# A fused attention, expert, scan and ternary layer stack: step sizes of the scan in one bundle, uncut steps, planner weights of its own for the first and last sequences, and three PSUM banks for the first attention

## The chip, the core and the metric

The kernel runs on one core of one Trainium2 chip. That core has five engines with a queue each: TensorE (PE, with weight loads, PEld, beside it), VectorE (DVE), ScalarE (ACT), GpSimd (POOL) and SyncE (SP), which issues the DMAs here. Each queue runs in order. The metric is the device time of one execution in microseconds (us).

## What is computed

Eight sequences of 512 rows by 256 columns go through four residual blocks. Cut to what matters:

```python
x = x + layernorm(attention(layernorm(x)))   # bf16, 2 heads, relu on q, k, v and output
x = x + layernorm(experts(layernorm(x)))     # 8 experts of 176 and a shared one, top 2 by sqrt(softplus(.)) + bias
x = x + layernorm(state_space(layernorm(x))) # f32, below
x = x + layernorm(ternary_ffn(layernorm(x))) # f32, hidden 1024, relu squared, rms norm

# state_space, per sequence: 512 channels, 16 states each, 512 time steps
z, xb, B, C, dt = split(h @ W_in.T)
delta = softplus(dt @ W_dt.T + 2 * b_dt)     # the step sizes
u = silu(conv4(repeat(xb)) + conv_b)
state = exp(delta * A) * state + delta * u * B
y = (sum(state * C) + u * D) * silu(z)
out = y @ W_out.T
```

## The kernel before, in words

**Chains.** The work of a sequence is cut into steps that are put into rounds: EARLY (attention, norms, the gate of the experts), LATE (experts, two norms, input projection, convolution, step sizes), GATE and BACK (z, gating, output projection, ternary layers, store). A round is begun only when every step of the round before it has been taken.

**The scan.** The 512 channels stand in four tiles of 128 partitions, with 16 states each: 64 scan steps per sequence, each over 128 x 512. For each, PE spreads a row of B over the partitions (L966), DVE multiplies it by `du` (L1437), ACT makes `exp(delta * A)` (L1171), DVE scans (L1430), POOL multiplies the state by C (L1453), and PE adds the product into `ps_y` (L973). After 16 of them, DVE takes the tile's sum (L1443, "taken").

**Planner.** `weave` writes each engine's order at build time. It walks a clock with a cost for every step (tables `BUSY` and `SCAN_BUSY`, in units of 10 ns). At each turn it gives the engine to the step that can start first; those that can start within one unit of it are told apart by urgency: the rest of a chain times a weight by eighth of the chain (`URGENT`, or `FIRST` for the first iteration), against a weight for the scan. The orders are fixed, and semaphores alone hold the engines together on the chip.

**Iterations.** Iteration n weaves the scan of sequence n, LATE of n+1, EARLY of n+2, BACK of n-1 and GATE of n. Iterations 1 to 4 are a loop, 0, 5, 6 and 7 are written out. Ahead of them EARLY of sequence 0 runs alone (with the quantising of the ternary weights beside it), then LATE of 0 is woven with EARLY of 1 until `du` of its tile 0 is planned; what is left of both is held over into iteration 0, where LATE of 1 and EARLY of 2 are begun only once both are through. After iteration 7, BACK of sequence 7 runs alone. Iteration 6 has no EARLY, iteration 7 neither EARLY nor LATE.

**Step sizes.** For each tile i there are ten steps: `d` (PE, L899), `d_abs` (ACT, two instructions, L1108 and L1109), `d_exp`, `d_one`, `d_less`, `d_log` (ACT, one each, L1112 to L1123), `d_fix`, `d_sum`, `delta`, `du` (POOL, L1477 to L1488). `d_log` needs another activation table than the exponentials. `d_abs` of tiles 0 to 2 waits until the scan of the sequence before has taken the same tile (`free_slot`, and `CROSS` in the planner); tile 3 has two slots in turn. The tiles come one after another, in the order 0, 3, 1, 2, each nine rounds after the last:

```python
    for i in range(CT):
        k = 15 + 9 * D_AT[i]
        steps += [(k, "P", ("d", i)), (k + 1, "A", ("d_abs", i)), (k + 2, "A", ("d_exp", i)), (k + 3, "A", ("d_one", i)),
```

**Halves.** `halved` gives the long steps (`proj`, `gram`, `fc`, `wout` on PE, `x4` and `apply` on ACT, `add` and `gate_root` on POOL, the store on SP) a first half `..._a`, so that the planner may put other work between. Matmuls and activations are the same in number either way; each POOL `add` and `gate_root` is two instructions of half the size, each store two DMAs of 256 KB.

**First attention.** In EARLY every product of PE goes into the one PSUM bank `XE`, and the next waits until ACT has copied the last out (`EARLY_BANK`).

Of the kernel before, what the change touches and what calls it, by code (L numbers as in the profile page):

```python
# [49 lines left out]


D_ORDER = (0, CT - 1) + tuple(range(1, CT - 1))
D_AT = tuple(D_ORDER.index(i) for i in range(CT))

# [103 lines left out]
def late_rounds():  # L158
# [30 lines left out]
def back_rounds():  # L189
# [8 lines left out]
    for t in range(NT):  # L198
        r += [[("P", ("proj", t))], [("P", ("gram", t))], [("A", ("p_out", t))]]
        if t == 2:  # L200
# [3 lines left out]
          [("V", ("o", "shift"))], [("A", ("o", "apply"))], [("G", ("o", "add"))], [("S", "store_a"), ("S", "store")]]  # L204
# [13 lines left out]
def quant_rounds():  # L218

    r = []  # L220
    for w in range(2):
# [3 lines left out]
        for h in range(2):  # L225
# [4 lines left out]

FIRST_HALF = {"proj": "proj_a", "gram": "gram_a", "fc": "fc_a", "wout": "wout_a", "x4": "x4_a", "apply": "apply_a", "add": "add_a",
              "gate_root": "gate_root_a"}


def first_half(e, step):

    if isinstance(step, str):
        return FIRST_HALF.get(step)
    name, i = step
    if name in FIRST_HALF:  # L240
        return FIRST_HALF[name], i
# [16 lines left out]
def places(rounds):  # L258

    at = {}  # L260
    for r in rounds:
        for e, step in r:
# [6 lines left out]
    "A": {"b_turned": 91, "back apply_a": 98, "back apply": 98, "c_out": 48, "cw_turned": 48, "d_abs": 114, "d_exp": 54, "d_less": 61,  # L269
          "d_log": 54, "d_one": 52, "dt_out": 48, "eps16": 19, "exp": 122, "f_turned": 48, "gate_abs": 17,  # L270
          "gate_exp": 12, "gate_log": 14, "h_turned": 91, "late apply_a": 94, "late apply": 94, "p_out": 38, "probs": 122, "pv_out": 48,
          "qk_out": 48, "raw": 48, "relu": 49, "round": 20, "shift": 123, "square": 53, "tanh": 49, "turned": 91,
          "v_out": 48, "v_relu": 96, "w_out": 48, "wo_out": 48, "wo_relu": 96, "x4_a": 112, "x4": 112, "x_one": 52, "x_tanh": 57,
          "x_turned": 91, "y_turned": 91, "z_tanh": 49},
    "G": {"add_a": 110, "add": 110, "d_fix": 123, "d_sum": 122, "delta": 122, "du": 123, "gate_root_a": 270, "gate_root": 270, "gated_y": 123,
          "rms": 98, "root": 98, "rstd": 98},
    "P": {"b_turn": 45, "bm": 70, "c": 130, "conv": 96, "cw_turn": 25, "d": 96, "down": 131, "dt": 130, "f_turn": 44,
          "fc_a": 96, "fc": 96, "gate": 60, "gram_a": 89, "gram": 89, "h_turn": 45, "proj_a": 173, "proj": 173, "pv": 86, "qk": 43, "scores": 22,
          "turn": 45, "up1": 45, "up3": 45, "v": 44, "weigh": 32, "wo": 44, "wout_a": 173, "wout": 173, "x_turn": 45, "xs": 130,
          "y_turn": 45, "z": 130},  # L280
    "V": {"add": 60, "aggr": 24, "b_hi": 34, "b_lo": 54, "b_mid": 20, "b_rest": 52, "back stats": 109, "center": 78,
          "divide": 78, "early stats": 130, "gate_eq": 33, "gate_gt": 34, "gate_low": 33, "gate_or": 33,
          "gate_rank": 31, "gate_sum": 11, "gate_twin": 18, "gated": 60, "gram_pick": 61, "late stats": 98,
          "max": 113, "ms": 60, "qk_bias": 53, "scale": 34, "silu": 60, "stats0": 66, "u": 66, "v_bias": 60,
          "weighted": 60, "wo_bias": 60, "z_silu": 60},
}
SCAN_BUSY = {"decay": 62, "spread": 33, "drive": 60, "scan": 114, "product": 123, "pair": 122, "sum": 96, "taken": 66, "load": 6}


TABLE_LOAD = 128  # L290
LOG_TABLE = ("log",)
USES = {"d_log": "log", "gate_log": "log", "d_exp": "exp", "gate_exp": "exp", "exp": "exp", "decay": "exp",
        "tanh": "tanh", "x_tanh": "tanh", "z_tanh": "tanh"}
# [13 lines left out]
def busy(e, kind, step):  # L307

    n, of = name_of(step), BUSY.get(e, {})
    return of.get(n, of.get(kind + " " + n, 6 if e == "S" else 9))  # L310
# [12 lines left out]
def scan_entries(e, j, part):  # L323
# [23 lines left out]
    elif e == "S" and part == 0 and (j < 0 or 1 <= j <= PER - 5):  # L347
# [11 lines left out]
FIRST = {"late": (42.9, 24.5, 7.37, 44.6, 3.04, 338, 3.77, 11),  # L359
          "early": (2.05, 15.5, 0.226, 0.444, 0.464, 5.13, 0.419, 47.2),  # L360
          "back": (0.342, 0.491, 0.571, 0.801, 0.855, 0.521, 0.922, 0.117),
          "scan": (134, 39.9, 69.3, 11.5, 39.2, 17, 25.5, 3.42)}
# [1495 lines left out]
```

## Time and profile before

| what | value |
|---|---|
| median of 3 runs | 1937.45 us (1933.76 to 1938.24) |
| the profiled execution | 1933.68 us |
| its span, first to last instruction | 1931.9 us |
| mean granted TensorE clock | 0.925 of full speed |
| PE busy | 1602.0 us (83%) |
| DVE busy | 1545.5 us (80%) |
| ACT busy | 1208.3 us (63%) |
| POOL busy | 1001.8 us (52%) |

Shares are means over stages with different limits; the table by stage stands with the rows below. First scans of iterations 0 to 7 are at 210.8, 429.5, 644.3, 860.9, 1069.5, 1281.2, 1492.2 and 1692.3 us; the last tile is taken at 1855.4 us.

### The profile page before, as it was taken

The page shows a single profiled execution, that of the slowest core. Times are in us where ns is not written, and L with a number is a line of the kernel's source. Part 1 is how long each engine was busy: PE and PEld are TensorE (multiplying, and loading weights), DVE is VectorE, ACT ScalarE, POOL GpSimd, SP SyncE. Part 2 cuts the span into 40 slices and gives each one's busy share as a digit, 9 for nine tenths or more (in the row PEclk, how much of TensorE's full clock was granted, in tenths as well). Part 3 has the DMA queues.
Part 4 walks back from the last instruction along what each step waited for, and adds up shares of the span by engine and source line. Part 5 has one row for each costly group of instructions (what it writes and reads, how often), then busy time and mean ns, then how long its engine had stood idle before and what let it go on. Part 6 is the DMA issues. An engine that isn't in the chain of part 4 may idle for free. (4 is left out here: it accounts for less than half of the span.)

```text
span 1931.9 us, 22676 instructions
## 1 busy us (share of the span) xinstructions
PE 1602.0 (83%) x5880; PEld 713.8 (37%) x5948; DVE 1545.5 (80%) x2808; ACT 1208.3 (63%) x2037; POOL 1001.8 (52%) x796
## 2 busy tenths in 40 slices
PE   2266688848998899878998899889997999889857
PEld 0113223323552346233542345233632363235325
DVE  6664799858998889978998889888997869986840
ACT  3447757767667694858577685769576538644322
POOL 0010764473368635773469535873568327964630
PEclk9768799869999899989999999899999999989988
DMA  5000232311233212321232222321233214332300
GB/s 161 1 6 26 84 114 68 107 33 63 72 103 113 80 63 72 130 95 66 67 115 104 82 66 88 117 90 60 66 116 111 72 41 127 119 124 95 111 31 12
DMA packets 94729, 157.95 MB, mean 82 GB/s; under 512 B 11068, under 2 KB 23788, under 8 KB 94596
## 3 DMA queue, kind: packets, MB, share of 16 engines
q1 hardware_dynamic: 94596, 156.43, 24.6%
q8 instruction: 52, 0.85, 0.2%
q14 instruction: 81, 0.66, 0.1%
HBM read 143.83 MB, written 12.58 MB: 81 GB/s over the span
## 5 line engine op out<-in xcount | busy, mean ns | idle before, releaser
L1453 POOL TENSOR_TENSOR prod<-state,c_all 128x512 f32<-128x512 f32 x512 | 650.8, 1278 | 537.4 <-DVE state L1430 447.5
L1430 DVE TENSOR_TENSOR_SCAN state<-decay,ps_b 128x512 f32<-128x512 f32 x512 | 622.4, 1216 | 32.3 <-POOL prod L1453 4.0
L973 PE MATMUL ps_y<-prod,idf 128*128 128x512 f32 x1024 | 591.5, 669 | 24.6 <-POOL prod L1453 18.8
L1171 ACT ACTIVATE decay<-delta,a_neg 128x512 f32<-128x512 f32 x512 | 364.2, 721 | 251.8 <-DVE state L1430 248.0
L1437 DVE TENSOR_TENSOR ps_b<-du,ps_b 128x512 f32<-128x512 f32 x512 | 348.3, 680 | 75.2 <-PE ps_b L966 70.9
L966 PE MATMUL ps_b<-b_rows,sel_b 48*128 48x512 bf16 x512 | 203.2, 402 | 77.2 <-DVE state L1430 75.6
L973 PEld LDWEIGHTS ps_y<-prod,idf 128*128 128x128 f32 x1024 | 169.3, 199 | 169.0 <-issue 107.2
L966 PEld LDWEIGHTS ps_b<-b_rows,sel_b 48*128 48x128 bf16 x512 | 46.5, 93 | 376.7 <-DVE state L1430 275.8
L830 PE MATMUL ps_x<-xT,w 128*128 128x512 bf16 (+1 forms) x386 | 128.8, 412 | 36.1 <-DVE arena_l L1336 13.6
L944 PE MATMUL ps_x<-arena_b,fcT 128*128 128x512 f32 x256 | 127.3, 612 | 1.1 <-ACT arena_b L1150 0.7
L950 PE MATMUL ps_x<-pjT,arena_b 128*128 128x256 f32 x512 | 119.9, 384 | 4.2 <-ACT arena_b L1159 2.8
L742 PE MATMUL ps_x<-hT,win 128*128 128x512 bf16 (+1 forms) x456 | 117.3, 393 | 2.7 <-DVE arena_l L1346 0.6
L950 PEld LDWEIGHTS ps_x<-pjT,arena_b 128*128 128x128 f32 x512 | 95.1, 190 | 24.8 <-ACT arena_b L1159 7.1
L1069 ACT ACTIVATE arena_l<-ps_x 128x512 f32<-128x512 f32 (+1 forms) x104 | 62.1, 598 | 58.1 <-PE ps_x L830 43.2
L1322 DVE SCALAR_TENSOR_TENSOR arena_l<-arena_l,ps_x 128x512 f32<-128x512 f32 (+1 forms) x104 | 70.2, 675 | 23.8 <-ACT arena_l L1069 23.5
L830 PEld LDWEIGHTS ps_x<-xT,w 128*128 128x128 bf16 (+1 forms) x416 | 36.0, 102 | 127.7 <-issue 59.7
L905 PE MATMUL ps_x<-wout,u 128*128 128x256 f32 x256 | 66.6, 419 | 10.7 <-POOL u L1506 10.5
L742 PEld LDWEIGHTS ps_x<-hT,win 128*128 128x128 bf16 (+1 forms) x480 | 45.7, 101 | 76.7 <-issue 27.4
L954 PE MATMUL ps_x<-arena_b 128*128 128x128 f32 x512 | 68.1, 281 | 0.0
L1326 DVE TENSOR_TENSOR arena_l<-arena_l,ps_x 128x512 f32<-128x512 f32 x88 | 59.6, 678 | 8.9 <-PE ps_x L838 8.6
L944 PEld LDWEIGHTS ps_x<-arena_b,fcT 128*128 128x128 f32 x256 | 46.5, 193 | 52.3 <-issue 34.8
L954 PEld LDWEIGHTS ps_x<-arena_b 128*128 128x128 f32 x512 | 62.0, 192 | 8.8 <-issue 6.5
(238 smaller groups left out, 2362.3 us busy)
## 6 DMA issues: line engine op xcount, KB each, us to landing
c_all<-c_rows SPq DMA_DIRECT2D x512, 256.0 KB
c_rows<-arena_l SPq DMA_DIRECT2D x32, 256.0 KB
out<-arena_b SPq DMA_DIRECT2D x16, 256.0 KB
x_in<-in_base SPq DMA_DIRECT2D x8, 256.0 KB
c_all<-in_winT SPq DMA_DIRECT2D x1, 1280.0 KB, 7.3
arena_b<-in_w_fc SPq DMA_DIRECT2D x1, 1024.0 KB, 6.9
arena_l<-in_w_proj SPq DMA_DIRECT2D x1, 1024.0 KB, 9.0
w<-in_w1T SPq DMA_DIRECT2D x1, 792.0 KB, 9.6
```

Of the source, the lines that this page charges most:

```text
L742: ins = nc.tensor.matmul(dst, win[:, k, part, lo:lo + n], rhs[:, k, :], start=(i == 0), stop=(i == 5))
L830: ins = nc.tensor.matmul(ps_x[0:m, bank, :], w[:, k, c * P:c * P + m], xT[:, k, :], start=(k == 0), stop=(k == KD - 1))
L944: ins = nc.tensor.matmul(ps_x[:, back_bank(s, i), :], fcT[:, k, i * P:(i + 1) * P], x3T[:, k, :], start=(k == 0), stop=(k == KD - 1))
L950: ins = nc.tensor.matmul(ps_x[:, back_bank(s, i), 0:D], hf[:, m, i * P:(i + 1) * P], pjT[:, m, :], start=(m == 0), stop=(m == FM - 1))
L954: ins = nc.tensor.matmul(ps_x[:, back_bank(s, i), D:D + P], hf[:, m, i * P:(i + 1) * P], hf[:, m, i * P:(i + 1) * P], start=(m == 0), stop ...
L966: nc.tensor.matmul(ps_b[:, n % NDB, :], sel_b[lo:lo + 48, st, :].broadcast_to([48, P]), b_rows[lo:lo + 48, s.par, ct // 2, :], start=True, ...
L973: nc.tensor.matmul(ps_y[:], idf[:], prod[:, n % NP, :], start=(n % NST == 0), stop=(n % NST == NST - 1)).then_inc(reduced, 1)
L1171: nc.scalar.activation(decay[:, n % NDA, :], delta[:, slot(s, ct), :], ACT.Exp, scale=a_neg[:, ct, st:st + 1]).then_inc(decayed, 1)
L1322: ins = stt(g, g, 1.0, ps_x[0:m, 0, :], ALU.add, ALU.mult)
L1430: nc.vector.tensor_tensor_scan(state[:, n % NS, :], decay[:, n % NDA, :], ps_b[:, n % NDB, :], 0.0, ALU.mult, ALU.add).then_inc(scanned, 1)
L1437: nc.vector.tensor_tensor(ps_b[:, j % NDB, :], du[:, slot(s, ct), :], ps_b[:, j % NDB, :], ALU.mult).then_inc(driven, 1)
L1453: nc.gpsimd.tensor_tensor(prod[:, n % NP, :], state[:, n % NS, :], c_all[:, n % NC, :], ALU.mult).then_inc(multiplied, 1)
```

## The change

**Step sizes in one bundle.** `D_ORDER` and `D_AT` go. The tiles come in the order 0, 1, 2, 3, their first rounds 14, 15, 17 and 18 in place of 15, 42, 51 and 24, so that the four tiles' steps share rounds. `d` of tile i now waits for `u` of i+1 (tile 3 for `d_abs` of tile 0) in place of `u` of tile 3.

**Uncut steps.** `halved` and everything ending in `_a` go; a POOL `add`, `gate_root` and the store are one instruction each.

**Planner.** `BUSY` is another table, the cost of loading an activation table is no longer counted apart (it lies in `d_exp`, `d_log` and `gate_log`), there are new weights `URGENT` and `FIRST`, and weights of their own for iteration 6 (`BUT_ONE`) and iteration 7 (`LAST`).

**Banks.** For sequence 0 the 22 products of the attention take the banks `XE`, 1 and 2 in turn, and wait for the copy three products back and for what they read.

```diff
-D_ORDER = (0, CT - 1) + tuple(range(1, CT - 1))
-D_AT = tuple(D_ORDER.index(i) for i in range(CT))
...
+    d0 = (14, 15, 17, 18)
     for i in range(CT):
-        k = 15 + 9 * D_AT[i]
+        k = d0[i]
...
-EARLY, LATE, BACK, QUANT, GATE = (halved(r) for r in (early_rounds(), late_rounds(), back_rounds(), quant_rounds(), gate_rounds()))
+EARLY, LATE, BACK, QUANT, GATE = early_rounds(), late_rounds(), back_rounds(), quant_rounds(), gate_rounds()
...
-URGENT = {"late": (1.07, 0.00728, 16.8, 1.59, 10.8, 0.0792, 0.106, 0.0435),
-          "early": (573, 12.7, 31.1, 1.48e+04, 2650, 36.1, 48.6, 3.13),
-          "back": (2.03, 102, 0.0246, 0.997, 0.832, 0.0938, 0.278, 0.712),
-          "scan": (3.58, 0.00555, 618, 1.07, 0.162, 0.27, 1e-05, 0.647)}
+URGENT = {"late": (0.32, 0.21, 0.17, 1.42, 0.34, 0.61, 0.01, 0.02),
+          "early": (10.39, 34.83, 6.82, 0.21, 3.35, 1.44, 0.16, 15.73),
+          "back": (17.26, 1.18, 330.85, 0.1, 0.06, 9.73, 0.79, 0.05),
+          "scan": (1.15, 30.65, 1781.42, 14, 0.66, 0.61, 1.19, 2.87)}
...
+def early_bank(s, step):
+
+    return (XE, 1, 2)[TURN_USES.index(step) % 3] if is_seq(s, 0) and step in TURN_USES else XE
...
+            bank = early_bank(s, step)
+            if is_seq(s, 0) and step in TURN_USES:
+                k = TURN_USES.index(step)
+                if k >= 3:
+                    eng.wait_ge(early["A"], ea(s, "A", EARLY_BANK[TURN_USES[k - 2]]))
...
-                if D_AT[i] == 0:
-                    eng.wait_ge(late["V"], la(s, "V", ("u", CT - 1)))
-                elif D_AT[i] == 3:
-                    eng.wait_ge(late["A"], la(s, "A", ("d_abs", D_ORDER[0])))
+                if i < 3:
+                    eng.wait_ge(late["V"], la(s, "V", ("u", i + 1)))
+                else:
+                    eng.wait_ge(late["A"], la(s, "A", ("d_abs", 0)))
...
-                h = slice(0, NT // 2) if i == "add_a" else slice(NT // 2, NT)
-                eng.wait_ge(back["A"], bk(s, "A", ("o", "apply_a" if i == "add_a" else "apply")))
-                ins = tt(x3[:, h], x3[:, h], tn[:, h], ALU.add)
+                eng.wait_ge(back["A"], bk(s, "A", ("o", "apply")))
+                ins = tt(x3, x3, tn, ALU.add)
...
-            urgent = FIRST if held else URGENT
+            urgent = FIRST if held else (URGENT, BUT_ONE, LAST)[max(0, 2 - left)]
...
-            late0.rest = [1e3 * x for x in late0.rest]
-            early1.rest = [1e6 * x for x in early1.rest]
+            late0.rest = [1e6 * x for x in late0.rest]
+            early1.rest = [1e9 * x for x in early1.rest]
```

## Rows read from the trace of the kernel before

**Rows 1.** Windows by stage: busy us of each engine, granted clock, DMA share, GB/s.

```profile
110.00:210.80 100.80, 69.61 (x314) 27.17 (x319) 54.75 (x154) 67.98 (x127) 11.26 (x10) 0.74 0.07 24
210.80:429.50 218.70, 162.15 (x538) 56.93 (x546) 183.73 (x326) 150.90 (x244) 136.12 (x105) 0.86 0.25 85
...
1492.20:1692.30 200.10, 181.69 (x612) 79.24 (x619) 162.16 (x251) 115.05 (x181) 114.97 (x94) 0.97 0.28 92
1692.30:1855.40 163.10, 145.67 (x413) 62.56 (x414) 128.46 (x174) 63.85 (x100) 93.75 (x76) 0.94 0.31 105
1855.40:1931.90 76.50, 47.89 (x200) 34.87 (x200) 8.19 (x39) 20.28 (x36) 10.06 (x9) 0.81 0.02 7
```

**Rows 2.** The same view, iterations 1 to 5 one by one; its sum.

```profile
sum 1062.70, PE 964.84 PEld 438.85 DVE 940.00 ACT 745.12 POOL 625.35; mean PE 192.97 PEld 87.77 DVE 188.00 ACT 149.02 POOL 125.07
```

**Rows 3.** The scan's line, and POOL's two kinds of steps: count, times.

```profile
L1430 DVE TENSOR_TENSOR_SCAN state<-decay,ps_b x512: 1178/1220/1222, 210.8 to 1850.7; 128x512 f32<-128x512 f32 x171
...
L1453 POOL TENSOR_TENSOR prod<-state,c_all 128x512 f32<-128x512 f32 x512 | 650.8, 1278 | 537.4 <-DVE state L1430 447.5 <-PE ps_y L973 84.8 <-DMA c_all<-c_rows 3.2
...
L1437 DVE TENSOR_TENSOR ps_b<-du,ps_b 128x512 f32<-128x512 f32 x512 | 348.3, 680 | 75.2 <-PE ps_b L966 70.9 <-POOL du L1488 3.5 <-issue 0.6
...
L1488 POOL TENSOR_TENSOR du<-delta,u 128x512 f32<-128x512 f32 x32 | 40.6, 1269 | 1.1
```

**Rows 4.** Windows over the last 60 us of iteration 4.

```profile
1264.50:1279.50 15.00, 11.52 (x26) 3.32 (x25) 9.99 (x14) 8.14 (x11) 14.87 (x13) 1.00 0.19 66
sum 60.00, PE 50.85 PEld 15.43 DVE 47.57 ACT 42.18 POOL 53.36; mean PE 12.71 PEld 3.86 DVE 11.89 ACT 10.54 POOL 13.34
```

**Rows 5.** Timeline, end of iteration 4: start us, us, engine, line, what.

```profile
1247.41 0.74 DVE L1443 SCALAR_TENSOR_TENSOR u<-u,dpar,ps_y 128x512 f32<-128x512 f32 x1
...
1267.95 0.69 ACT L1108 ACTIVATE arena_l<-ps_x,b 128x512 f32<-128x512 f32 x1 [1.64 <-PE ps_x L899]
...
1277.86 1.27 POOL L1488 TENSOR_TENSOR du<-delta,u 128x512 f32<-128x512 f32 x1
```

**Rows 6.** What DVE waited for on PE in iterations 1 to 6.

```profile
DVE ps_b L1437 <- PE ps_b L966: 37.6, 30, 3.6
```

**Rows 7.** Timeline of the last BACK: projection, and the first norm's apply and add.

```profile
1869.70 2.07 ACT L724 ACTIVATE arena_b<-arena_b,sh_w,rs_w 128x256 f32<-128x256 f32 x4 [3.39 <-DVE sh_w L717]
1870.87 2.27 POOL L1502 TENSOR_TENSOR arena_b<-x,arena_b 128x512 f32<-128x512 bf16 x2 [1.40 <-ACT arena_b L724]
...
1903.83 3.62 PE L950 MATMUL ps_x<-pjT,arena_b 128*128 128x256 f32 x16
```

**Rows 8.** Timeline of DVE and POOL, 219 to 224 us.

```profile
221.28 0.65 DVE L1246 TENSOR_TENSOR g<-g,gb 128x32 f32<-128x32 f32 x1
...
220.62 1.26 POOL L1453 TENSOR_TENSOR prod<-state,c_all 128x512 f32<-128x512 f32 x1
```

**Rows 9.** Timeline ahead of the first scan.

```profile
194.28 0.75 DVE L1358 SCALAR_TENSOR_TENSOR u<-ps_x,cb,u 128x512 f32<-128x512 f32 x1
...
199.72 0.69 ACT L1108 ACTIVATE arena_l<-ps_x,b 128x512 f32<-128x512 f32 x1 [3.22 <-PE ps_x L899]
...
206.06 1.28 ACT L1171 ACT_TABLE_LOAD   x1
208.70 1.34 ACT L1171 ACTIVATE decay<-delta,a_neg 128x512 f32<-128x512 f32 x2 [1.36 <-POOL delta L1484]
...
209.98 5.78 POOL L1466 TENSOR_TENSOR g<-g,half 128x16 f32<-128x16 f32 x2
```

**Rows 10.** Timeline of ACT: the gate's last step of EARLY of sequence 1.

```profile
261.09 0.57 ACT L1051 COPY cwT<-ps_x 24x512 bf16<-24x512 bf16 x1 [1.44 <-PE ps_x L812]
```

**Rows 11.** Timeline of the first attention.

```profile
17.36 1.04 PE L769 MATMUL ps_x<-arena_e,wq 128*128 128x512 bf16 x2 [0.68 <-ACT arena_e L992]
...
29.28 0.69 DVE L1217 TENSOR_TENSOR arena_e<-arena_e,bvo 128x1024 bf16<-128x1024 bf16 x1
...
30.00 1.06 ACT L1012 ACTIVATE arena_e<-arena_e 128x1024 bf16<-128x1024 bf16 x1 [5.83 <-DVE arena_e L1217]
```

More of the change, by code:

```diff
@@ L268 @@
 BUSY = {
[L269 to L285, printed above, removed]
-}
@@ L287 @@
[L287 to L293, printed above, removed]
+    "A": {"apply": 196, "probs": 110, "v_relu": 110, "wo_relu": 110, "round": 30, "d_one": 52, "d_less": 52, "f_turned": 48, "p_out": 37, "relu": 48, "square": 52, "w_out": 48, "z_tanh": 49, "cw_turned": 48,
+          "exp": 122, "gate_abs": 15, "gate_exp": 12, "gate_log": 142, "pv_out": 47, "qk_out": 47, "raw": 47, "turned": 90,
+          "v_out": 47, "wo_out": 47, "x_turned": 106, "y_turned": 89, "b_turned": 89, "c_out": 48, "d_abs": 114,
+          "d_exp": 180, "d_log": 182, "dt_out": 48, "h_turned": 89, "tanh": 49, "x4": 224, "x_one": 52, "x_tanh": 58},
@@ new lines @@
+    "G": {"add": 225, "rms": 98, "rstd": 98, "root": 98, "gate_root": 541, "delta": 122, "du": 122, "d_fix": 122, "d_sum": 122, "gated_y": 122},
+    "P": {"f_turn": 44, "fc": 172, "gram": 178, "proj": 345, "wout": 345, "z": 130, "cw_turn": 22, "gate": 60, "pv": 86,
+          "qk": 43, "scores": 22, "turn": 45, "v": 44, "wo": 87, "x_turn": 45, "y_turn": 45, "b_turn": 45, "bm": 70, "c": 130,
+          "conv": 86, "d": 86, "down": 152, "dt": 130, "h_turn": 45, "up1": 43, "up3": 43, "weigh": 32, "xs": 130},
@@ L294 @@
+SCAN_BUSY = {"decay": 62, "spread": 33, "drive": 60, "scan": 114, "product": 125, "sum": 87, "taken": 66, "load": 6}
 HANDOVER = 12
@@ L307, in busy @@
 def busy(e, kind, step):
-    n, of = name_of(step), BUSY.get(e, {})
-    return of.get(n, of.get(kind + " " + n, 6 if e == "S" else 9))
+    n = name_of(step)
+    if kind == "early" and n == "shift":
+        return 60 if e == "V" else 110
+    return BUSY.get(e, {}).get(n, 6 if e == "S" else 9)
 CROSS = {("early", "y_turned"): ("late", -1, ("up3", MCH - 1)), ("early", "cw_turned"): ("late", -1, ("weigh", MCH - 1)),
@@ L407, in weave @@
     port = {"V": 0, "G": 0}
-    table = ("exp", "tanh")
     done, order = {}, {e: [] for e in "PAVGS"}
@@ L447, in weave @@
             for op, n, _ in scan_entries(e, j, part):
-                if op in USES and USES[op] not in table:
-                    when, table = when + TABLE_LOAD, ("exp", "tanh")
                 when += SCAN_BUSY[op]
@@ L453, in weave @@
         else:
-            uses = USES.get(name_of(st[3])) if e == "A" else None
-            if uses is not None and uses not in table:
-                when, table = when + TABLE_LOAD, LOG_TABLE if uses == "log" else ("exp", "tanh")
             when += busy(e, st[0], st[3])
@@ L479 @@
               "cw_turn": "gate_abs"}
+TURN_USES = [step for step in EARLY_BANK if step[0] in ("qk", "v", "scores", "turn", "pv", "wo")]
+READS = {"qk": lambda i: "x_turned", "v": lambda i: "x_turned", "pv": lambda i: ("turned", 2 * i + 1), "wo": lambda i: ("pv_out", 1)}
+def early_bank(s, step):
+    return (XE, 1, 2)[TURN_USES.index(step) % 3] if is_seq(s, 0) and step in TURN_USES else XE
 def sandwich(nc, base, wqT, bq, wkT, b_k, wvT, bv, woT, bo, gateT, gate_b, w1T, w3T, w2T, winT, wdtT, b_dt,
@@ L919, in back_pe @@
                 ins = project(ps_x[:, XB, :], ZC + i * P, P, hT[:, s.par])
[L920 removed]
+            elif name == "wout":
                 if i == 0:
@@ L986, in early_act @@
             act = nc.scalar.activation
+            source = ("qk" if name == "qk_out" else "scores" if name == "raw" else "turn" if name == "turned" else name[:-4], i)
+            bank = early_bank(s, source)
             if name == "x_turned":
@@ L1497, in back_pool @@
             elif name == "w":
-                h = slice(0, NT // 2) if i == "add_a" else slice(NT // 2, NT)
-                eng.wait_ge(back["A"], bk(s, "A", ("w", "apply_a" if i == "add_a" else "apply")))
-                if i == "add_a":
-                    wait(eng, out_stored, s.count(PER, 0))
-                ins = tt(x3[:, h], x2[:, s.par, h], tn[:, h], ALU.add)
+                eng.wait_ge(back["A"], bk(s, "A", ("w", "apply")))
+                wait(eng, out_stored, s.count(PER, 0))
+                ins = tt(x3, x2[:, s.par], tn, ALU.add)
             elif name == "gated_y":
@@ L1536, in back_sync @@
         def back_sync(eng, s, step):
-            h = slice(0, NT // 2) if step == "store_a" else slice(NT // 2, NT)
-            eng.wait_ge(back["G"], bk(s, "G", ("o", "add_a" if step == "store_a" else "add")))
-            eng.dma_start(seq_rows(out, s)[:, h], x3[:, h]).then_inc(out_stored, PER // 2)
+            eng.wait_ge(back["G"], bk(s, "G", ("o", "add")))
+            eng.dma_start(seq_rows(out, s), x3).then_inc(out_stored, PER)
         def scan_sync(eng, s, j, part):
```

165 lines of the change are left out of this document (78 added, 87 removed).

## The prediction

> **What bounds the kernel now.** I read the stages first, then the waits, then the seam between two iterations. The stages: 100.8 us of the second half of the prologue, eight iterations, and a last BACK of 76.5 us in which PE is busy for 47.9 and DVE for 8.2 [rows 1]. What the reader is to see is that no engine is idle for long in the middle: over iterations 1 to 5 (1062.7 us, 212.5 each) PE is busy for 193.0 and DVE for 188.0 of each, ACT for 149, POOL for 125 [rows 2]. So an iteration can't go below 193, and what a plan can win or lose there is the 19.5 us (PE) or 24.5 us (DVE) that are open. Each scan step costs DVE 1.22 + 0.68 = 1.90 us and POOL 1.28 [rows 3].
>
> POOL's share of 0.59 misleads. In the last 60 us of iteration 4 it is busy for 53.4, in the last 15 for 14.87, while DVE is busy for 47.6 and 9.99 [rows 4]. There the step sizes of the next sequence meet the scan on POOL: the third tile is taken at 1247.4, the last `du` ends at 1279.1, and the next iteration's first scan is at 1281.2 [rows 5]. The scan and LATE end together, and POOL is the engine that both need.
>
> **The change, part by part.** Sums are against the profiled execution's 1933.7 us (a span of 1931.9 and 1.8 around it), which lies 3.8 us under the median.
>
> *Banks of the first attention.* A product takes 1.04 us and PE stands still for 0.68 between two of them, for the copy [rows 11]. With three banks those 0.68 go, 20 times at most (13.6 us, one bound). But the copies don't wait for PE alone: the bias on v is made by DVE at 29.28, behind the splitting of the weights, and ACT waits 5.83 us for it before it may go on to the scores [rows 11]. So the first six products gain nothing. Later the next limit is ACT's own queue, and only where ACT waited for a turn or a score behind a copy is something won, some four times 0.5. I take **-2** (bounds -13.6 and 0).
>
> *Ahead of the first scan.* `d` of tile 0 now needs `u` of tile 1 only, which ends at 195.0, in place of the fourth; `d` takes about 2 us, so `d_abs` starts at 197.2 in place of 199.72: -2.5 [rows 9]. But the plan ahead of the scan runs until the round that holds `du` of tile 0 (22) is through, and this round now comes with everything of the other tiles up to it. Ahead of `d_log` of tile 0 that is `d_abs` twice, `d_exp`, `d_one`: 6 ACT instructions of 0.69, 4.1 us. Behind it and before the first decay stand 11 more (7.6 us), and since logarithms and exponentials now alternate, 4 more table loads of 1.28 (5.1 us) [rows 9]. The load before the first decay ended at 207.3; it will at 207.3 - 2.5 + 4.1 + 12.7 = 221.6, and the first scan goes from 210.85 to about 222.4, **+11.5** (from +9, if two logarithms fall together, to +12).
>
> The Trainium skill (ScalarE: Activation LUTs, What ACT_TABLE_LOAD costs) puts a switch at 1.28 us for the load and some 1.38 for a drain; by it the four extra loads would be 10.6 us and not 5.1. The trace agrees on the load and shows no drain behind it, so nothing is added for it.
>
> *Iteration 0.* In exchange, less is held over. The gate of sequence 1 now ends only at 261.1 [rows 10], since each of its small DVE steps waits behind a scan; LATE of 1 can't begin before. After the change the gate's DVE steps run while ACT works off the bundle, with no scan about. What is left are POOL's 16 steps of 1.27 and a `gate_root` of 5.8 [rows 3, 9], 26 us from about 204 on, and some products: LATE of 1 begins near 235, 26 us earlier. Then DVE is the limit: 183.7 us of work in the iteration [rows 1] less about 3 of the gate, at the share of iterations 1 to 5 (188.0 / 212.5 = 0.885) 204 us in place of 218.7: **-15** (bounds -28 at a share of 0.95, and 0). The front as a whole: -3.5.
>
> *Iterations 1 to 5, the bundle.* `d_abs` of tile 2 waits for the third take, and in the bundle it stands in round 18. Every POOL step of the step sizes stands in round 19 or later, so all 16 come behind that take: 20.3 us, with the 12 to 14 products that are left (17 us) and two `gated_y` (2.5 us) 40 us, against the 33.8 from that take to the next first scan now [rows 3, 5]. Now only tiles 1 (its end) and 2 stand there. In full this is 8 POOL steps too many, 10.2 us. Two things give back: ahead of the take POOL is free of those 8 steps, and the scan may be up to 4 us further; and the last POOL steps are needed only by later tiles, so they can lie under the next iteration. I take **+3** each (bounds -4 and +10).
>
> *Iterations 1 to 5, uncut steps.* A `proj` holds PE for 3.6 us [rows 7] where a half held it for 1.8, and the B row of the next scan waits behind it, with DVE behind that. DVE's wait for this row is 37.6 us in iterations 1 to 6, 6.3 each [rows 6]: between 0 and a doubling. POOL's `gate_root` becomes one instruction of 5.8 us, and an `add` one of 2.3; products queue behind them, but POOL is idle for 87 us of the iteration. I take **+1** each (bounds 0 and +6).
>
> Here a rule speaks against the change. In the trace a DVE step of 128x32 that else takes 0.18 took 0.65, and ended when the product beside it on POOL ended [rows 8]. The Trainium skill (SBUF — State Buffer, Who interferes with whom) calls it an exclusive lock: a DVE instruction with two SBUF inputs waits out the POOL instruction that holds the shared port. The trace agrees in this row. By it an uncut `gate_root` could hold one DVE step up to 2.9 us longer in each sequence.
>
> *The weights.* No row can price an urgency. Bounds are the open 19.5 us below, and as much above; I take 0 for iterations 1 to 5. Those of iteration 6 (PE busy for 181.7 of 200.1) and 7 (145.7 of 163.1, [rows 1]) are for chains that are there and not for an average: iteration 7 at iteration 6's PE share of 0.908 is 160.5. I take -3 for each; with bundle and uncut steps iteration 6 is **+1**, iteration 7 **-3**.
>
> *The last BACK.* Nothing runs beside it. `apply` ends at 1871.77; the half `add` began at 1870.87 beside it and both ended at 1873.1 [rows 7]. Uncut it begins at 1871.8 and takes 2.27: +1.0, and the same for the last one. The store then sends 512 KB at once where half was already on its way: 0 to 1.5, I take 0.8. **+2.8**.
>
> Sum: -2 - 3.5 + 5 x 4 + 1 - 3 + 2.8 = +15.3, so 1949 against the profiled execution; with half of the 3.8 us to the median, 1950.
>
> **The rivals.**
> - *The bundle shortens LATE and DVE closes up* (the other side). LATE is as long as the iteration, and its last third is four serial tiles with DVE idle for 12.4 of the last 60 us [rows 4]. If the scan uses the 28 us ahead of the third take for two more steps, the burst shrinks and an iteration loses 4 us: 6 x -4 - 5.7 = -30, 1904. It decides if the third take moves from 178 us after the first scan to 172 or less. Against it: POOL had no room left behind the take.
> - *Only the ends move.* The plans come out equal in the middle: -2 - 3.5 - 3 - 3 + 2.8 = -9, 1925, or with a few us lost in the middle 1931 to 1943.
> - *The POOL burst in full.* +10 in each of six iterations and the rest as above: 1933.7 + 60 - 6 = 1988. For it speaks that POOL is at 14.87 of 15 already; against it, that POOL is at half load in the next iteration's start.
>
> **How the numbers follow.** Forecast (1943 to 1965) 0.33; the burst dearer than that 0.22; the middle a wash (1931 to 1943) 0.12; only the ends 0.13; the bundle pays 0.20. A change within 0.3% (5.8 us, about what a measurement of this kernel can tell) is the third: same 0.12, slower 0.55, faster 0.33. Both signs hold much, so the range takes in the rival at 1904 and most of the burst: 1905 to 1982. That of the forecast alone is 1943 to 1965.
>
> **What the profile after would show.** The first scan near 222, with log and exp loads alternating ahead of it; the first `tanh` of LATE of 1 near 235 and not after 261; in iterations 1 to 5 no `d_fix` ahead of the third take, then POOL full for some 40 us; iterations of 216 or 217 us; more DVE wait for the B row; the last `add` in one piece, 1 us later. It would be wrong if the weights move an iteration by more than 5 us either way, which no row can exclude, or if the gate isn't through before the scan begins.

## The result and the profile after

| | before | after |
|---|---|---|
| median of 5 runs | 1937.45 us (1933.76 to 1938.24) | 1921.95 us (1911.96 to 1922.44) |
| the profiled execution, its span | 1933.68, 1931.9 us | 1922.44, 1920.6 us |
| mean granted TensorE clock | 0.925 | 0.906 |
| ratio, 95% interval | | 0.9907, 0.9884 to 0.993 |

The kernel became 0.9% faster; 1950, slower, was forecast. The time lies inside the range and beside the rival "only the ends move" (1925). That rival's number is right, but its reason, plans that come out equal in the middle, is not: the experiments below show parts of 13, 5 and -19 us an iteration that nearly cancel. First correct one slip of the text above: before the change the first rounds of tiles 0 to 3 were 15, 33, 42 and 24, nine rounds apart in the order 0, 3, 1, 2; "15, 42, 51 and 24" is wrong. No number hangs on it.

From the first scan of each iteration comes a table by stage, in us; the first column is what lies ahead of the first scan.

| | first scan | it. 0 | it. 1 to 5 | it. 6 | it. 7 | last BACK |
|---|---|---|---|---|---|---|
| before | 210.8 | 218.7 | 1062.7 | 200.1 | 163.1 | 76.5 |
| after | 220.0 | 200.1 | 1061.1 | 202.1 | 157.5 | 79.8 |
| difference | +9.2 | -18.6 | -1.6 | +2.0 | -5.6 | +3.3 |
| forecast | +9.5 | -15 | +20 | +1 | -3 | +2.8 |

Every column but one is within 4 us of its forecast. The miss is iterations 1 to 5: -1.6 where +20 was forecast. Windows by stage of the kernel after (columns as in [rows 1]), which answer to [rows 1]:

```profile
220.00:420.10 200.10, 164.43 (x544) 59.03 (x545) 179.60 (x314) 135.09 (x225) 123.92 (x97) 0.86 0.27 91
...
1481.20:1683.30 202.10, 187.10 (x619) 82.53 (x619) 158.83 (x251) 114.63 (x181) 115.53 (x92) 0.91 0.27 91
1683.30:1840.80 157.50, 145.39 (x414) 63.21 (x414) 128.46 (x174) 63.29 (x100) 93.55 (x74) 0.93 0.32 109
1840.80:1920.60 79.80, 48.63 (x200) 35.07 (x200) 8.27 (x40) 20.30 (x36) 9.78 (x7) 0.81 0.02 7
```

And the sum of the same view over iterations 1 to 5, which answers to [rows 2]:

```profile
sum 1061.10, PE 975.93 PEld 441.54 DVE 921.89 ACT 739.20 POOL 622.74; mean PE 195.19 PEld 88.31 DVE 184.38 ACT 147.84 POOL 124.55
```

The work is nearly the same: POOL 124.6 of each iteration (125.1 before), DVE 184.4 (188.0), PE 195.2 (193.0). What changed is where it lies. Windows of iteration 4, cut at its takes: to the first, to the second, to the third, and to the next iteration's first scan. First the kernel before:

```profile
1069.50:1147.00 77.50, 72.13 (x263) 32.41 (x267) 69.46 (x124) 62.31 (x116) 30.45 (x25) 0.98 0.22 74
1147.00:1208.30 61.30, 59.74 (x332) 35.45 (x331) 58.46 (x141) 33.51 (x61) 32.18 (x25) 1.00 0.27 88
1208.30:1247.40 39.10, 33.47 (x85) 10.82 (x85) 34.09 (x44) 31.66 (x49) 32.20 (x27) 0.95 0.35 117
1247.40:1281.20 33.80, 27.22 (x56) 8.62 (x57) 25.88 (x38) 21.43 (x33) 30.26 (x25) 0.91 0.26 87
```

Then the kernel after; the last row is a part of the last stretch.

```profile
1058.90:1127.90 69.00, 64.52 (x211) 27.54 (x209) 63.23 (x109) 47.24 (x87) 30.57 (x24) 0.94 0.23 79
1127.90:1181.00 53.10, 52.86 (x248) 30.28 (x247) 47.87 (x86) 32.43 (x59) 22.25 (x19) 1.00 0.25 83
1181.00:1231.70 50.70, 48.64 (x222) 22.31 (x222) 45.41 (x103) 39.35 (x70) 34.28 (x25) 1.00 0.32 109
1231.70:1271.50 39.80, 30.22 (x63) 9.57 (x64) 28.36 (x48) 28.79 (x41) 37.39 (x31) 0.79 0.25 85
1244.90:1262.00 17.10, 13.01 (x19) 3.67 (x20) 13.29 (x21) 12.94 (x18) 17.10 (x15) 0.50 0.23 74
```

Read the four stretches one by one. Behind the third take POOL is busy for 37.39 of 39.80: the burst is there, 6.0 us longer than the 33.8 of before [rows 5], and PE, 76% busy in it, falls to half its clock for 17.1 us. But the third take comes 172.8 us after the iteration's first scan, where it came at 177.9 before; ahead of it PE is busy for 166.0 of 172.8 (96%), before for 165.3 of 177.9 (93%). The burst costs 6 us and the stretch ahead of it gives 5.1 back. Over iterations 1 to 5 the two balance: the third take comes at 171.7 in place of 177.6 on average, and 40.5 us follow it in place of 34.9. The profile can't say which edit does either; the experiments below can.

The timeline of iteration 4's end, kernel after, answers to [rows 5]:

```profile
1231.71 0.74 DVE L1424 SCALAR_TENSOR_TENSOR u<-u,dpar,ps_y 128x512 f32<-128x512 f32 x1
1232.18 1.27 POOL L1456 TENSOR_TENSOR arena_l<-arena_l 128x512 f32<-128x512 f32 x1
...
1262.68 2.49 POOL L1434 TENSOR_TENSOR prod<-state,c_all 128x512 f32<-128x512 f32 x2
1265.12 1.27 POOL L1467 TENSOR_TENSOR du<-delta,u 128x512 f32<-128x512 f32 x1
1266.34 1.27 POOL L1463 TENSOR_TENSOR delta<-du,delta 128x512 f32<-128x512 f32 x1
1266.46 0.75 DVE L1424 SCALAR_TENSOR_TENSOR u<-u,dpar,ps_y 128x512 f32<-128x512 f32 x1 [3.90 <-PE ps_y L953]
1267.83 1.26 POOL L1467 TENSOR_TENSOR du<-delta,u 128x512 f32<-128x512 f32 x1 [0.22 <-POOL delta L1463]
```

The first of the 16 step-size steps on POOL (L1456, `d_fix`) starts 0.5 us after the third take, so all 16 lie behind it, as foreseen. But the scan's last two products go ahead of the last step sizes, and the fourth take follows them at 1266.46 while POOL still works on `delta` and `du`.

### The profile page after: what moved, and what is told of

Its sections match the earlier page's. It is cut to its first block and busy times, and to the rows that moved or that the text cites. A ratio compares the mean times of both kernels' runs of the same rounds, so it can differ in the third digit from the quotient of the medians.

```text
span 1920.6 us, 22705 instructions
## 1 busy us (share of the span) xinstructions
PE 1619.2 (84%) x5948; PEld 723.3 (38%) x5948; DVE 1524.5 (79%) x2808; ACT 1199.9 (62%) x2035; POOL 998.4 (52%) x772
## 5 line engine op out<-in xcount | busy, mean ns | idle before, releaser
L953 PE MATMUL ps_y<-prod,idf 128*128 128x512 f32 x1024 | 611.6, 690 | 19.9 <-DVE u L1424 10.2
L946 PE MATMUL ps_b<-b_rows,sel_b 48*128 48x512 bf16 x512 | 209.5, 413 | 74.7 <-DVE state L1411 73.8
L953 PEld LDWEIGHTS ps_y<-prod,idf 128*128 128x128 f32 x1024 | 176.6, 205 | 170.5 <-issue 110.7
L818 PE MATMUL ps_x<-xT,w 128*128 128x512 bf16 (+1 forms) x416 | 136.0, 412 | 23.1 <-DVE arena_l L1317 10.7
L910 PE MATMUL ps_x<-wout,u 128*128 128x256 f32 x256 | 71.5, 442 | 17.7 <-POOL u L1483 17.6
L723 PEld LDWEIGHTS ps_x<-hT,win 128*128 128x128 bf16 (+1 forms) x480 | 44.7, 100 | 81.8 <-issue 23.2
L1134 ACT ACTIVATE arena_b<-ps_x 128x512 f32<-128x512 f32 x64 | 38.6, 602 | 55.1 <-PE ps_x L925 55.1
L910 PEld LDWEIGHTS ps_x<-wout,u 128*128 128x128 f32 x256 | 56.0, 224 | 32.7 <-POOL u L1483 21.3
```

Source lines behind the costliest of these rows:

```text
L723: ins = nc.tensor.matmul(dst, win[:, k, part, lo:lo + n], rhs[:, k, :], start=(i == 0), stop=(i == 5))
L818: ins = nc.tensor.matmul(ps_x[0:m, bank, :], w[:, k, c * P:c * P + m], xT[:, k, :], start=(k == 0), stop=(k == KD - 1))
L910: ins = nc.tensor.matmul(half_bank(back_bank(s, i), t), u[:, s.par, ct, t * P:(t + 1) * P], wout[:, ct, :], start=(ct == 0), stop=(ct == C ...
L946: nc.tensor.matmul(ps_b[:, n % NDB, :], sel_b[lo:lo + 48, st, :].broadcast_to([48, P]), b_rows[lo:lo + 48, s.par, ct // 2, :], start=True, ...
L953: nc.tensor.matmul(ps_y[:], idf[:], prod[:, n % NP, :], start=(n % NST == 0), stop=(n % NST == NST - 1)).then_inc(reduced, 1)
```

## The experiments

Four kernels cross the two orders of the step sizes with the two sets of weights. The table of costs, the halves and the banks stay with the kernel that each starts from; no run changes the costs alone.

**1. The kernel before with the bundle alone.** Order, rounds and waits of `d` as in the change; weights, halves and bank as before.

```diff
-D_ORDER = (0, CT - 1) + tuple(range(1, CT - 1))
+D_ORDER = tuple(range(CT))
...
-        k = 15 + 9 * D_AT[i]
+        k = (14, 15, 17, 18)[i]
```

> The kernel before with one part of the change: the four tiles' step sizes in one bundle (order 0, 1, 2, 3, first rounds 14, 15, 17, 18, and the waits of d that go with it). Costs, halves and weights are those of before. Theory A (the bundle gives back ahead of the third take what POOL's burst costs behind it): the third take comes some 4 to 8 us earlier in an iteration and the stretch from it to the next first scan is as much longer, iterations 1 to 5 stay within 1.5 us of 212.5 each; the front alone gains, first scan at 219 to 222 and iteration 0 at 198 to 206; the whole 1925 to 1935. Theory B (the bundle costs what was forecast and the new weights win it back): iterations 1 to 5 at 216 to 222 each, the whole 1945 to 1980.

Measured: 2017.06 us, ratio 1.0406 (1.0381 to 1.0432). Iterations 1 to 5 take 225.9 on average, +13.4 each, more than either theory allowed. Windows of its iteration 4, cut at the takes like those above:

```profile
1110.50:1180.50 70.00, 63.96 (x226) 26.86 (x228) 67.38 (x120) 56.03 (x104) 30.56 (x25) 1.00 0.26 83
1180.50:1251.80 71.30, 67.17 (x367) 39.87 (x370) 56.07 (x149) 38.79 (x72) 33.88 (x25) 0.98 0.22 71
1251.80:1291.20 39.40, 34.78 (x88) 11.46 (x88) 34.52 (x42) 25.74 (x42) 24.68 (x21) 0.99 0.37 127
1291.20:1335.40 44.20, 33.22 (x54) 9.90 (x55) 25.94 (x39) 28.34 (x40) 37.75 (x31) 0.70 0.19 66
```

The last stretch has 44.2 in place of 33.8: +10.4, near the 10.2 us of eight POOL steps that the prediction named and then marked down to 3. But the trace counts otherwise: behind the third take stand 16 step-size steps and 12 products where nine and 13 stood before, six instructions more. POOL is busy for 7.5 us longer (37.75 against 30.26), and idle for 2.9 longer; that the sum comes to 10.4 is luck. The third take comes at 180.7 in place of 177.9: +2.8. Together this is iteration 4's 13.2. The bundle by itself is a loss.

**2. The kernel after with the serial order** (0, 3, 1, 2, nine rounds apart, waits and banks of `d` to match); all else as after.

```diff
-    d0 = (14, 15, 17, 18)
+    d0 = (15, 33, 42, 24)
```

> The kernel after with the step sizes put back one tile after another (order 0, 3, 1, 2, nine rounds apart, waits as before); all else as after. Theory A: the first scan comes back to 211 and iteration 0 to 215 or more, iterations 1 to 5 stay within 1.5 us of 212; the whole near 1930. Theory B: iterations 1 to 5 fall to 204 to 208 each, since the new weights keep what they win and POOL's burst is gone; the whole 1895 to 1915. Theory C (weights fit one set of chains, and any other pairing loses whatever the part is worth): iterations 1 to 5 at 216 or more.

Measured: 1994.88 us, ratio 1.0293 (1.0268 to 1.0317); iterations 1 to 5 sum to 1116.4, 223.3 each, +55.3 in all against after. The serial order is no better under these weights either (theory C). The stretch behind the third take is 44.7 in iteration 4, longer than with the bundle (39.8), though only 12 of the 16 step-size steps lie in it: how many steps stand in the burst doesn't by itself set its length. The first scan is at 215.9, where 211 was expected.

**3. The kernel before with the weights of after** (`URGENT`, `FIRST`, `BUT_ONE`, `LAST`).

```diff
-            urgent = FIRST if held else URGENT
+            urgent = FIRST if held else (URGENT, BUT_ONE, LAST)[max(0, 2 - left)]
```

> The kernel before with the weights of after (URGENT, FIRST, and BUT_ONE and LAST for iterations 6 and 7), nothing else. Theory A says nothing of the middle here. Theory B: the weights are what wins, iterations 1 to 5 at 204 to 208. Theory C: 215 or more each, and iteration 7 under 160.

Measured: 1979.05 us, ratio 1.0206 (1.0184 to 1.0229); iterations 1 to 5 sum to 1103.0, +40.3, 8.1 each. All of it lies ahead of the third take, which comes at 187.4 in iteration 4 (177.9 before); the stretch behind it has 32.2 (33.8). Iteration 7 takes 161.3; under 160 was expected.

**4. The kernel after with the weights of before** in every iteration.

```diff
-            urgent = FIRST if held else (URGENT, BUT_ONE, LAST)[max(0, 2 - left)]
+            urgent = FIRST if held else URGENT
```

> The kernel after with the weights of before in every iteration. Theory B: iterations 1 to 5 at 217 to 222. Theory C: the same or worse, so that B and C are told apart only by the other three: under C all four crossed pairings lose 4 us or more in each of iterations 1 to 5; under A the two pairings that change the bundle alone lose nothing. In all of them the front follows the bundle: first scan near 220 with it, near 211 without.

Measured: 2052.71 us, ratio 1.0587 (1.0564 to 1.0611); iterations 1 to 5 sum to 1154.1, 93.0 more than after, 18.6 each. In iteration 4 the third take comes at 185.5 and the stretch behind it has 43.5; with the weights of after they are 172.8 and 39.8. So of 16.4 us in that iteration 12.7 lie ahead of the take and 3.7 behind it.

All four crossed pairings lose 2 to 6%: neither set of weights is good by itself, only for the chains that it goes with. Experiments 1 and 4 have the same bundle and the same weights, yet 4 takes 4.9 us more in an iteration. Of what differs between them, the new costs and the uncut steps bear on the middle, and no run tells the two apart. So the way from before to after is +13.4 (bundle), +4.9 (costs and uncut steps), -18.6 (weights): -0.3 an iteration.

What do the new weights do? Two suspects were tried by themselves: that LATE no longer stands still ahead of the take, and that the scan's products go first in the burst. ACT's timeline around the third take of iteration 4, first the kernel of experiment 1, then the kernel after (the third `ACTIVATE` pair of each bundle, `d_abs` of tile 2, waits for the take):

```profile
1268.83 0.68 ACT L1109 ACTIVATE delta<-ps_x,b 128x512 f32<-128x512 f32 x1
...
1291.96 0.69 ACT L1108 ACTIVATE arena_l<-ps_x,b 128x512 f32<-128x512 f32 x1 [0.57 <-DVE u L1443]
```

```profile
1223.58 0.71 ACT L1090 ACTIVATE delta<-ps_x,b 128x512 f32<-128x512 f32 x1
...
1232.54 0.69 ACT L1089 ACTIVATE arena_l<-ps_x,b 128x512 f32<-128x512 f32 x1 [0.56 <-DVE u L1424]
```

In experiment 1 `d_abs` of tile 1 is done at 1269.5, and that of tile 2 follows 22.5 us later; after, 8.2 us later. The old weights hurried LATE to a place where it could only wait, while the scan, which it waited for, was late.

**5. Experiment 1 with a second slot of `delta` for tile 2**, so that `d_abs` of tile 2 needn't wait for the take (its `d_log` does, for the slot of `du`). For room, eight small scratch tensors lie in the space of `decay`.

```diff
-    CROSS[("late", ("d_abs", ct))] = ("taken", -1, ct)
+    CROSS[("late", ("d_abs" if ct < CT - 2 else "d_log", ct))] = ("taken", -1, ct)
...
-        delta, du = (sb(n, [P, CT + 1, T]) for n in ("delta", "du"))
+        delta, du = sb("delta", [P, CT + 2, T]), sb("du", [P, CT + 1, T])
```

> The kernel before with the bundle (as in the first experiment), and with a second slot for tile 2 of delta, so that d_abs of tile 2 no longer waits for the third take; d_log of tile 2 still does. Eight of the sixteen POOL steps can then stand ahead of that take. Weights, costs and halves are those of before. Theory A (the loss of 12 to 13 us an iteration with the bundle alone is POOL's burst behind the third take): iterations 2 to 5 fall from 224 to 226 to 213 to 217, the stretch from the third take to the next first scan from 44 to some 34. Theory B (the bundle loses for its longer rounds, whatever the take does): they stay at 222 or more.

Measured: 1984.2 us, ratio 1.0245 (1.0222 to 1.0268). Iterations 2 to 5 average 219.9 (225.7 in experiment 1), and in iteration 4 the stretch behind the take is 35.6 in place of 44.2, though the take itself comes 3.6 later, at 184.3. The wait for the take is part of the bundle's price under the old weights, 5.8 of some 13 us, and not all of it: 213 to 217 was expected if it were all, 222 or more if none.

**6. The kernel after, its long steps executed as halves.** The plan is the one of after, step by step; each long step is issued as its two halves, one right behind the other, and the store as two.

```diff
-            for item in order[e]:
+            for item in in_halves(order)[e]:
```

> The kernel after in its own planned order, step for step, but each long step is again carried out as its two halves, one right behind the other: the POOL adds and gate_root as two instructions, the store as two DMAs; only what may overlap changes. Theory A (uncut steps cost at the very end only): the tail from the last take falls from 79.8 to 76.5 to 77.5, iterations by no more than 0.5 us each, the whole by 2.5 to 5 us. Theory B (one long POOL instruction is cheaper than two, and holds DVE less often): DVE busy rises by 1 to 3 us an iteration and the whole stays or gets slower.

Measured: 1913.3 us (1907.53 to 1913.57), ratio 0.9867 (0.985 to 0.9884). Iterations 1 to 5 sum to 1058.6 (1061.1 after), the last BACK has 76.5 in place of 79.8. It is the fastest kernel of the study. What uncut steps cost in execution is the 3.3 us at the end, where `add` and store overlap nothing; in the middle no cost of theirs shows where +1 for each iteration was forecast: experiments 7 and 8, uncut and with the same plan, sum to 1055.3 and 1054.3 there. What the planner loses or wins by having no halves to place isn't tested by this. The last row of the stage windows above is after's last BACK; the intervals of the two kernels only touch, so that halves are faster as a whole is likely, and that they aren't slower is shown.

**7. The kernel after with one bank in the first attention.**

```diff
-    return (XE, 1, 2)[TURN_USES.index(step) % 3] if is_seq(s, 0) and step in TURN_USES else XE
+    return XE
```

> The kernel after with one PSUM bank for the first attention again. Theory A (DVE and ACT queues hide it): 1.5 to 3 us slower, all of it ahead of the first scan. Theory B (each of 20 handovers counts): 8 to 13 us slower.

Measured: 1918.18 us (1912.41 to 1926.63), ratio 0.9909 (0.9887 to 0.993). The first scan is at 221.9 in place of 220.0: the banks are worth 1.9 us, 2 forecast. The whole time can't tell it, since iterations with the very plan of after came out up to 3.9 us shorter here (the last section shows why).

**8. The kernel after with the common `URGENT` in iterations 6 and 7** (`FIRST if held else URGENT`).

> The kernel after with the weights URGENT in iterations 6 and 7 as well, FIRST kept in iteration 0. Theory A (weights for the chains that are there): iteration 6 at 204 to 208 in place of 202, iteration 7 at 160 to 164 in place of 157.6, the whole 4 to 12 us slower. Theory B (the 5.5 us of iteration 7 come from the bundle's state at its start): no change beyond 1 us.

Measured: 1920.03 us, ratio 0.9914 (0.9896 to 0.9931). Iteration 6 takes 203.5 and iteration 7 161.1. Against the 202.1 and 157.5 of after, and the 198.4 and 155.9 that experiments 6 and 7 both show in these iterations, own weights are worth 1.4 to 5 us in iteration 6 and 3.6 to 5 in iteration 7. The whole doesn't show it, since the middle, with the plan of after, came out 6.8 us shorter; "4 to 12 us slower" was expected.

**9 and 10. The scan's weight in its last eighth**, on which it hangs who goes first in the burst: raised in experiment 1, lowered in the kernel after.

```diff
-          "scan": (3.58, 0.00555, 618, 1.07, 0.162, 0.27, 1e-05, 0.647)}
+          "scan": (3.58, 0.00555, 618, 1.07, 0.162, 0.27, 1e-05, 5)}
...
-          "scan": (1.15, 30.65, 1781.42, 14, 0.66, 0.61, 1.19, 2.87)}
+          "scan": (1.15, 30.65, 1781.42, 14, 0.66, 0.61, 1.19, 0.1)}
```

> The kernel of the first experiment (before with the bundle) with one number changed: the scan's weight in the last eighth of an iteration is 5 and not 0.647, so that in the burst behind the third take POOL multiplies the scan's states ahead of the last step sizes (the last three of the sixteen come behind the last scan steps, as in after). Nothing ahead of the third take moves in the plan. Theory A (the loss is the order in the burst: with step sizes first the scan is late and nothing can hide its end): the stretch from the third take to the next first scan falls from 44 to 38 to 40, iterations 2 to 5 from 224 to 226 to 219 to 221, the whole to 1980 to 1995. Theory B (the loss is that other engines have nothing left to do in the burst): the stretch stays at 43 or more, the whole at 2010 or more.

> The kernel after with the reverse edit: the scan's weight in the last eighth of iterations 1 to 5 is 0.1 and not 2.87; the step sizes now go ahead of the last products. Nothing ahead of the third take moves in the plan. Theory A: the stretch from the third take to the next first scan grows from 37 to 40 to 42 to 46, iterations 1 to 5 from 212 to 216 to 219, the whole to 1940 to 1955. Theory B: no change beyond 1.5 us in an iteration, the whole 1915 to 1925.

Measured, 9: 2012.87 us, ratio 1.0404 (1.0379 to 1.0428); the stretch behind the third take of iteration 4 goes from 44.2 to 41.8 (44.9 to 42.7 on average), iterations 1 to 5 from 1129.7 to 1124.0, 1.1 each. The whole time doesn't show it (1.0406 in experiment 1), and 1980 to 1995 was expected. Measured, 10: 1928.06 us, ratio 0.9936 (0.9912 to 0.9959); iterations 1 to 5 sum to 1070.7, +9.6, and the stretch goes from 39.8 to 43.1 (40.5 to 43.7 on average). POOL's timeline at the end of iteration 4 of kernel 10 shows the order turned round, beside the one of after above:

```profile
1264.63 1.26 POOL L1467 TENSOR_TENSOR du<-delta,u 128x512 f32<-128x512 f32 x1
1265.85 4.93 POOL L1434 TENSOR_TENSOR prod<-state,c_all 128x512 f32<-128x512 f32 x4
1274.04 1.26 POOL L1483 TENSOR_TENSOR u<-u,arena_b 128x512 f32<-128x512 f32 x1 [3.26 <-DVE u L1424]
```

Four products wait behind the last `du`, the fourth take behind those. Products ahead of the last step sizes is the better order in both kernels, by 2.2 us of this stretch in the one and 3.2 in the other: real, and small. The greater part of the 18.6 us lies ahead of the take (12.7 of 16.4 in iteration 4).

**11. Experiment 6 with the slot of experiment 5**, the candidate for something faster still.

> After in its own plan with the long steps carried out in halves (the sixth experiment) and with the second slot for tile 2 of delta (the fifth); weights are those of after, so the plan moves only behind tile 2's d_abs. Theory A (with the weights of after LATE comes to the bundle only 9 us ahead of the third take, so that the slot frees little): within 3 us an iteration of the sixth experiment either way, the whole 1905 to 1925. Theory B (the slot is worth the 6 us an iteration that it gave in the fifth experiment): iterations 1 to 5 at 205 to 207, the whole 1880 to 1890.

Measured: 1923.01 us (1920.79 to 1929.21), ratio 0.9923 (0.9909 to 0.9936): slower than experiment 6 (0.9867), with intervals that don't meet. Under the new weights LATE stands still for 8 us only, so that there is little for the slot to free: one of the 16 POOL steps moves ahead of the third take. And the plan came out with the step sizes further ahead: in the first 23 us behind the third take of iteration 4 POOL begins four of the scan's products, where it begins seven in experiment 6. The stretch has 43.0 in place of 39.7. So the slot wasn't tried with the better order of the burst.

## Why the prediction was wrong, point by point

- **The weights, taken as 0 for iterations 1 to 5: the step that failed.** "No row can price an urgency" was right, and 0 was put in the middle of bounds of 19.5 us either way. On the bundle they are worth -18.6 an iteration (experiment 4), more than the 5 us that the prediction itself named as the sign that it is wrong. On the chains of before the same weights cost +8.1 (experiment 3: 40.3 / 5). The weights and the chains aren't two terms to be added; they are one.
- **The bundle at +3: too low as well, and the two misses hid each other.** With the weights of before it costs 13.4, above the bound of +10 (experiment 1). "8 POOL steps too many" was one too many (nine step-size steps stood there already), and one product fewer stands there now; the 40 us that the prediction added up for the whole burst are the 39.8 of after. What failed were the "two things" that give back. The scan didn't go further ahead of the take but came 2.8 us later, and the last POOL steps didn't slip under the next iteration. With the weights of after the first comes to pass: the third take moves from 177.9 to 172.8. The second doesn't: the last `du` ends at 1269.1, ahead of the next first scan at 1271.5; but the last step sizes lie beside the fourth take, and the burst has 39.8. The average over iterations 1 to 5, 171.7, meets the "172 or less" at which the rival "the bundle shortens LATE" was to decide, and still the iteration comes out even (-0.3 each), not 4 us ahead: the scan came further ahead of its third take, as that rival has it, but the burst didn't shrink.
- **Uncut steps, +1 an iteration: nothing in execution.** Experiment 6 runs the same plan in halves and its middle is 0.5 us an iteration shorter, less than equal plans differ by (the last section). The other table of costs wasn't a term of the prediction at all; with uncut steps in the plan it is +4.9 an iteration under the old weights (experiments 1 and 4). The wait for the B row did grow as foreseen, which the view of the waits over iterations 1 to 6 of the kernel after shows, answering to [rows 6]:

```profile
DVE ps_b L1418 <- PE ps_b L946: 55.8, 72, 3.8
```

- It went from 37.6 us (30 times) to 55.8 (72 times), +3.0 an iteration, while DVE's busy time fell by 3.6. Most of it, 14.4 of 18.2 us, is the plan's and not the uncut execution's: with the same plan in halves it is 52.0 us (72 times), so that carries 0.6 us an iteration at most.
- **The exclusive lock** between a POOL instruction and a DVE step (Trainium skill, SBUF — State Buffer, Who interferes with whom). `gate_root` is one instruction of 5.4 us after, and if it held DVE for long in each sequence, halves would show it. DVE is busy for 184.4 an iteration uncut and 184.1 in halves, and for 184.1 and 184.0 in experiments 7 and 8, which are uncut: no price of it shows.
- **Ahead of the first scan, +11.5 less 2: right** (+9.2). ACT's timeline there shows the loads and the first `tanh` of LATE of 1, whose start was forecast near 235 and is at 231.4; the gate's last step, at 261.1 in [rows 10], is at 219.9:

```profile
214.89 1.28 ACT L1104 ACT_TABLE_LOAD   x1
217.97 1.28 ACT L1152 ACT_TABLE_LOAD   x1
219.26 0.72 ACT L1152 ACTIVATE decay<-delta,a_neg 128x512 f32<-128x512 f32 x1
219.89 0.56 ACT L1033 COPY cwT<-ps_x 24x512 bf16<-24x512 bf16 x1
231.41 0.60 ACT L1051 ACTIVATE arena_l<-ps_x 128x512 f32<-128x512 f32 x1 [0.95 <-POOL du L1467]
```

- The load at 217.97 ends at 219.25, and the activation starts at 219.26. The Trainium skill's drain of some 1.38 us per switch (ScalarE: Activation LUTs, What ACT_TABLE_LOAD costs) isn't here. An estimate by that page: its drain, for the four extra loads, would have put the first scan 5.5 us later than forecast. With one bank it was forecast at 222.4 and is at 221.9 (experiment 7); with the bundle and nothing else of the change it is at 221.0 (experiment 1).
- **Iteration 0, -15: right in sign and near in size** (-18.6; the share of DVE is 179.60 of 200.10, 0.898 where 0.885 was taken). The cause is the bundle only in part: alone it gives -10.4 (208.3, experiment 1), and with the new costs and uncut steps but the old weights -3.4 (215.3, experiment 4). `FIRST`, which the prediction didn't price, carries the rest.
- **Iterations 6 and 7, +1 and -3: within 3 us** (+2.0 and -5.6). Experiment 8 shows that own weights gain in both. But the +2.0 of iteration 6 is no reading of its sign: with the same plan it took 198.4 in experiment 7, less than the 200.1 of before.
- **The banks, -2: right** (experiment 7, 1.9). The copies still wait for the bias on v, which DVE makes at 29.00 (29.28 in [rows 11]).
- **The last BACK, +2.8: right** (+3.3). The first `add`, uncut, stands whole behind `apply`, where before its half ran beside it [rows 7]; timeline of the last BACK, kernel after:

```profile
1855.12 2.07 ACT L705 ACTIVATE arena_b<-arena_b,sh_w,rs_w 128x256 f32<-128x256 f32 x4 [3.39 <-DVE sh_w L701]
1857.28 2.13 POOL L1479 TENSOR_TENSOR arena_b<-x,arena_b 128x1024 f32<-128x1024 bf16 x1 [2.38 <-ACT arena_b L705]
```

What stays open: how much of the 4.9 us between experiments 1 and 4 is the table of costs and how much the steps without halves, and what either is worth under the new weights. Also whether the serial order, with halves, and weights searched for it anew, iteration by iteration, would beat the bundle. Experiments 2 and 3 pair it with weights made for something else and can't tell. Nor was it tried which of the 32 weights of the middle carry the 12.7 us ahead of the take in iteration 4.

## What to carry to other kernels

Where an order is planned at build time from weights, a change of the chains and a change of the weights are to be costed as one: one without the other lost 2 to 6% here, the whole change won 0.9%. When the size of a term can't be read from any row, the forecast shouldn't rest on a zero for it; what can be read is how far an engine is from full ahead of the wait that decides (PE 93% before, 96% after), and that is the room for such a gain. Price a burst in full first, by counting what stands in it now and what will, and take off only what a row shows to have a place elsewhere.

## What the hardware showed unexpectedly

The granted TensorE clock falls in the middle of a kernel whose PE is busy for 84% of the time. Behind the third take PE waits for POOL; busy for 30.2 of 39.8 us there, it has a granted clock of 0.50, which is 1.2 GHz, for 17.1 us of iteration 4 (the window from 1244.9 above), against 0.94, 1.00 and 1.00 in the three stretches ahead. Ahead of the take there are two more low stretches, the end of one that began before the iteration (5.0 us in it) and one of 3.4. Before the change the low stretches of iteration 4 were of 3.4, 3.4 and 6.8 us. In experiment 7, whose plan there is the same as after, they are of 6.8 and 6.8 us, in experiment 8 there is one of 17.1, all behind the third take.

Equal plans give unequal times, and the traces show where. Iterations 1 to 5 have the same order of work on ACT, DVE and POOL in the kernel after and in experiments 7 and 8, and sum to 1061.1, 1055.3 and 1054.3 us. From the first take on they agree: 53.1 us to the second (53.2 in iteration 5), 50.7 to the third, and behind it 39.8 in iteration 4 of all three. What differs is the stretch from the first scan to the first take, and it goes with how long the granted clock is 0.50 in it:

| iteration | at 0.50 | length of the stretch |
|---|---|---|
| 4 of experiments 7 and 8 | 0 | 65.0, 65.0 |
| 1 of all three | 3.4 | 66.2, 66.2, 66.2 |
| 2 of all three | 6.8 | 67.0, 67.0, 67.0 |
| 5 of all three | 6.8 | 67.0, 67.7, 67.0 |
| 3 of experiments 7 and 8 | 4.3 | 68.1, 67.9 |
| 4 of after | 8.5 | 69.0 |
| 3 of after | 11.3 | 70.4 |

Iteration 3 of experiments 7 and 8 shows that the place of the low stretch counts too. These stretches explain 5.6 and 6.5 of the 5.8 and 6.8 us between the sums. In them PE and DVE are both nearly full (60.2 and 62.1 of 65.0 in experiment 7). Behind the third take, where POOL is what is full, the low clock costs nothing: experiment 7 has 13.7 us of it in iteration 4, after and experiment 8 have 17.1, and all take 39.8. An estimate from these numbers: with no low clock ahead of the first take, iterations 1 to 5 of the kernel after would take 14.6 us less (339.6 less five times 65.0).

The five times of the kernel after spread over 10.5 us, from 1911.96 at a mean clock of 0.919 to 1922.44 at 0.906. That the same makes this spread is likely and not shown, since one of the five has a trace; the mean clock alone doesn't tell it, as the longest of experiment 7's six times, 1926.63, has 0.918. A difference of a few us between two such kernels is read from single stages, not from the whole.
